# A four-layer decoder: the first projection rotates by a lane shuffle, and the fp4 rounding of all eight weight pieces stands beside it

## What is computed

```python
x = x + _L0_attn_ref(_layernorm(x), Wq, Wk, Wv, Wo)          # 16 heads of 32, 8 key heads
#   q = q * cos + _rotate_half(q) * sin ; k likewise
#   att = 50 * tanh(q k^T / 16 / 50), causal, softmax, times v, times Wo
x = x + _L0_xattn_ref(_layernorm(x), ctx, ctx)
x = x + _L0_ffn_ref(_layernorm(x), up_kernel, up_bias, down_kernel, down_bias)

def quantize_to_mxfp4(w, block_size=32):     # blocks of 32 along K
    amax = max(abs(block)); scales = exp2(floor(log2(max(amax, 1e-30))) - 2)
    idx = digitize(abs(w / scales), [0.25, 0.75, 1.25, 1.75, 2.5, 3.5, 5.0])
    q = sign(w / scales) * [0, .5, 1, 1.5, 2, 3, 4, 6][idx]
    return q, scales                          # the matmul uses q * scales
```

## Time and profile before

| | us |
|---|---|
| median of 3 runs (1390.68 to 1394.52) | 1392.82 |
| the profiled execution | 1394.05 |
| its span | 1392.3 |
| TensorE busy | 1239.9 (89%) |
| VectorE busy | 817.3 (59%) |
| ScalarE busy | 526.3 (38%) |
| GpSimd busy | 329.8 (24%) |
| load of the fp4 kernels, issue to landing (2560 KB) | 16.9 |

### The profile page before, as it was taken

One profiled execution on the slowest core, in us unless ns is written; L12 is line 12 of the kernel. 1 busy time (PEld: TensorE's weight loads), 2 busy tenths in 40 slices (PEclk: granted clock), 3 DMA queues, 4 the chain that ended last, 5 costly groups with the idle time before them and its releaser, 6 DMA issues. The chain is left out here.

```text
span 1392.3 us, 23432 instructions
## 1 busy us (share of the span) xinstructions
PE 1239.9 (89%) x9322; PEld 744.2 (53%) x9334; DVE 817.3 (59%) x2109; ACT 526.3 (38%) x967; POOL 329.8 (24%) x364
## 2 busy tenths in 40 slices
PE   5678779788999899899998998999999999994898
PEld 2246554456854544556664544555555555663455
DVE  2887767757687344768766766343111126777955
ACT  1019335563524433544444545111111114445453
POOL 0225502100003100245542221232222223450200
PEclk9688899998999999999999999999999999996999
DMA  9000000000040030000000000123232210000000
GB/s 384 1 0 3 1 1 2 0 1 1 1 197 2 10 112 1 1 2 3 3 2 1 2 2 1 52 75 95 80 106 80 84 37 1 2 3 0 1 1 31
DMA packets 13340, 48.02 MB, mean 34 GB/s; under 512 B 1688, under 2 KB 4888, under 8 KB 12464
## 3 DMA queue, kind: packets, MB, share of 16 engines
q1 hardware_dynamic: 13232, 46.53, 10.0%
HBM read 45.37 MB, written 1.15 MB: 33 GB/s over the span
## 5 line engine op out<-in xcount | busy, mean ns | idle before, releaser
L821 ACT ACTIVATE PT<-PS 128x384 f32<-128x384 f32 (+1 forms) x320 | 153.2, 531 | 189.3 <-PE PS L631 138.4
L1930 PE MATMUL PS<-HT,WA 128*128 128x512 f32 x448 | 201.5, 593 | 2.4 <-DVE MO L2008 2.0
L2008 DVE TENSOR_TENSOR MO<-PS,AO 128x512 f32<-128x512 f32 x56 | 38.7, 690 | 205.9 <-ACT AO L1998 205.8
L1930 PEld LDWEIGHTS PS<-HT,WA 128*128 128x128 f32 x448 | 84.7, 190 | 87.7 <-issue 82.9
L1998 ACT ACTIVATE AO<-PS 128x512 f32<-128x512 f32 x56 | 33.3, 597 | 247.9 <-PE PS L1930 247.9
L757 DVE CUSTOM_DVE_ANT_0 junk<-PS,TRI 128x128 bf16<-128x128 f32 (+1 forms) x384 | 112.6, 352 | 4.0 <-PE PS L612 0.2
L1938 PE MATMUL PS<-WA,HO 128*128 128x256 f32 x448 | 105.6, 378 | 0.0
L1938 PEld LDWEIGHTS PS<-WA,HO 128*128 128x128 f32 x448 | 84.5, 189 | 34.7 <-issue 24.9
L240 PE MATMUL PS<-identb 128*128 128x512 bf16 x388 | 99.2, 394 | 3.2 <-PEq L584 1.2
L2063 POOL TENSOR_TENSOR HO<-MO,GR 128x512 f32<-128x512 f32 x44 | 57.8, 1314 | 168.7 <-PE PS L1938 168.7
L612 PE MATMUL PS<-KS,QM 32*128 32x128 f32 (+1 forms) x768 | 86.7, 347 | 7.5 <-DVE QM L791 6.6
(11 more groups left out here) (323 smaller groups left out, 2412.8 us busy)
## 6 DMA issues: line engine op xcount, KB each, us to landing
WA<-w2f_in SPq DMA_DIRECT2D x28, 384.0 KB, 4.5
WA<-wl_in SPq DMA_DIRECT2D x1, 5137.0 KB, 16.0
GR<-gate_rows SPq DMA_DIRECT2D x20, 256.0 KB, 3.9
GB<-gate_rows SPq DMA_DIRECT2D x8, 512.0 KB, 7.4
WA<-wa_in SPq DMA_DIRECT2D x2, 1792.0 KB, 12.2
WB<-wb_in SPq DMA_DIRECT2D x1, 3208.0 KB, 18.4
WA<-wa_in SPq DMA_DIRECT2D x1, 2560.0 KB, 16.9
GR<-gate_rows SPq DMA_DIRECT2D x4, 448.0 KB, 4.0
```

The costliest lines, as they stand in the source:

```text
L821: act.activation(PT[:, g % 3, st_slot(k), 0:W], PS[:, st_bank(g, k), 0:W], ACT.Exp, scale=scale).then_inc(S["at_exp"], 1)
L1930: last = pe.matmul(PS[:, 2 * c + half, :], chunk(i, half)[:, k * P:(k + 1) * P], HT[:, k, c * CH:(c + 1) * CH], start=k == 0, stop=k == KD ...
```

## The change

The swapped weights are gone. In `project` TensorE computes each item once; VectorE takes it from PSUM with a shuffle that exchanges the two halves of each 32 lanes into RS, and multiplies it by the cosines into RC; GpSimd multiplies RS by the sines and adds. RC, RS and the PSUM banks of the items have four buffers. The products for V stand between the items from the third on, and GpSimd's wait for `b_in` stands behind its work.

All eight pieces are rounded in `project`. VectorE takes the largest magnitudes behind items 1 to 3 and forms all powers at once in four small instructions; ScalarE writes absolute values into H; with item m + 4 VectorE scales piece m and makes four of the seven comparisons, each into a bf16 tile of its own (0, 0.5, 1 or 2), and GpSimd makes the other three; TensorE sums the seven tiles by products with the identity (two items later); VectorE has put signs and powers together (one item later) and multiplies the sums by them, to bf16. The rounded pieces are turned by 32 bf16 products in the tail of the stage and copied by ScalarE. The attention keeps its own work alone, and the cross-attention has no kernel head, so that it takes the branch with the 24 `warm` matmuls.

The core of the diff:

```diff
@@ project, TensorE @@
-                    for n, (a, ap, _, j, c) in enumerate(work):
+                    for n, (a, _, j, c) in enumerate(work):
                         if n < NCH:
                             norm["columns"](pe, 2 * n + 1)
-                        if n >= 2:
-                            pe.wait_ge(S["rope_sin"], d["rope_sin"] + n - 1)
-                        for half, wt in enumerate((a, ap)):
+                        if n >= 4:
+                            pe.wait_ge(S["rope_pair"], d["rope_pair"] + n - 3)
+                            pe.wait_ge(S["rope_cos"], d["rope_cos"] + n - 3)
+                        for k in range(KD):
+                            last = pe.matmul(PS[:, n % 4, :], a[:, k, j * P:(j + 1) * P],
+                                             HT[:, k, c * CH:(c + 1) * CH], start=k == 0, stop=k == KD - 1)
+                        last.then_inc(S["proj"], 1)
+                        t = n - 2
+                        if 0 <= t < TT:
...
+                        kernels["tensor"](pe, n, NW)
@@ project, VectorE @@
-                        dve.tensor_tensor(tm(RC), ps(0), cos.to_broadcast([P, nchunk, T]), ALU.mult).then_inc(S["rope_cos"], 1)
-                        dve.tensor_tensor(tm(RS), ps(1), sin.to_broadcast([P, nchunk, T]), ALU.mult).then_inc(S["rope_sin"], 1)
+                        if n >= BUF:
+                            dve.wait_ge(S["rope_sum"], d["rope_sum"] + n - BUF + 1)
+                        dve.stream_shuffle(RS[:, n % BUF], ps, PAIR[hd]).then_inc(S["rope_pair"], 1)
+                        dve.tensor_tensor(wide(RC[:, n % BUF]), wide(ps), cos.to_broadcast([P, nchunk, T]),
+                                          ALU.mult).then_inc(S["rope_cos"], 1)
+                        kernels["vector"](dve, n, NW)
@@ project, GpSimd @@
+                        pool.tensor_tensor(wide(RS[:, n % BUF]), wide(RS[:, n % BUF]), sin.to_broadcast([P, nchunk, T]),
+                                           ALU.mult).then_inc(S["rope_sin"], 1)
+                        pool.wait_ge(S["rope_sin"], d["rope_sin"] + n + 1)
+                        pool.wait_ge(S["rope_cos"], d["rope_cos"] + n + 1)
+                        pool.tensor_tensor(dst[:, j, c * CH:(c + 1) * CH], RC[:, n % BUF], RS[:, n % BUF], ALU.add).then_inc(S["rope_sum"], 1)
+                        kernels["beside"](pool, n, NW)
                     pool.wait_ge(S["b_in"], 64)
@@ quantise_fp4 @@
+        STEPS = [(5.0, 2.0), (3.5, 1.0), (2.5, 1.0), (1.75, 0.5), (1.25, 0.5), (0.75, 0.5), (0.25, 0.5)]
+        OWN = 4
+        def largest(dve, m):
+            if m == 0:
+                dve.wait_ge(S["kernels_in"], 16)
+            dve.tensor_reduce(per(0, m), grp(piece(order[m])), AX, ALU.max, apply_absolute_value=True).then_inc(S["q_largest"], 1)
+        def scaled(dve, m):
+            dve.wait_ge(S["q_sizes"], m + 1)
+            v = grp(at["scaled"][:, m % 4])
+            dve.tensor_tensor(v, v, wide(per(2, m)), ALU.mult).then_inc(S["q_scaled"], 1)
+        def sizes(act, m):
+            if m >= 4:
+                act.wait_ge(S["q_steps"], OWN * (m - 3))
+                act.wait_ge(S["q_steps_beside"], (len(STEPS) - OWN) * (m - 3))
+            act.activation(at["scaled"][:, m % 4], piece(order[m]), ACT.Abs).then_inc(S["q_sizes"], 1)
+        def signed(dve, m):
+            dve.scalar_tensor_tensor(u32(grp(at["signed"][:, m % 2])), u32(grp(piece(order[m]))), 0x80000000, u32(wide(per(1, m))), ALU.bitwise_and,
+                                     ALU.bitwise_or).then_inc(S["q_signed"], 1)
+        def steps_of(eng, m, lo, hi, name):
+            eng.wait_ge(S["q_scaled"], m + 1)
+            if m >= 2:
+                eng.wait_ge(S["q_summed"], m - 1)
+            for j in range(lo, hi):
+                eng.tensor_scalar(at["steps"][:, m % 2, j, :], at["scaled"][:, m % 4], STEPS[j][0], STEPS[j][1], ALU.is_ge, ALU.mult).then_inc(S[name], 1)
+        def summed(pe, m):
+            pe.wait_ge(S["q_steps"], OWN * (m + 1))
+            pe.wait_ge(S["q_steps_beside"], (len(STEPS) - OWN) * (m + 1))
+            for j in range(len(STEPS)):
+                last = pe.matmul(PS[:, 6 + m % 2, :], identb[:], at["steps"][:, m % 2, j, :], start=j == 0, stop=j == len(STEPS) - 1)
+            last.then_inc(S["q_summed"], 1)
+        def kept(dve, m):
+            dve.wait_ge(S["q_summed"], m + 1)
+            dve.wait_ge(S["q_signed"], m + 1)
+            dve.tensor_tensor(rounded(m), PS[:, 6 + m % 2, :], at["signed"][:, m % 2], ALU.mult).then_inc(S["q_kept"], 1)
...
+            if n == last - 1:
+                pe.wait_ge(S["ctx_copied"], TT // 2)
+                for g in range(4):
+                    turned_over(pe, g)
+                for m in range(early - 2, early):
+                    summed(pe, m)
+                for g in range(4, 8):
+                    turned_over(pe, g)
@@ capped_attention, VectorE @@
-                        beside(dve, g, NQ)
@@ layers @@
-        cross_attention(32, norm=norm, head=kernels)
+        cross_attention(32, norm=norm)
```

More of the change, by code:

```diff
@@ new lines, in quantise_fp4, with begin @@
+        at = {}
+        rounded = lambda m: piece(order[m]).bitcast(BF16)[:, 0:CH]
+        def begin(tmp):
+            at.update(scaled=H[:].rearrange("p (j t) d -> p j (t d)", j=4), signed=tmp("SP", [P, 2, CH]), steps=tmp("IND", [P, 2, 7, CH], BF16),
+                      small=tmp("SM", [P, 3, early * NG]))
+        STEPS = [(5.0, 2.0), (3.5, 1.0), (2.5, 1.0), (1.75, 0.5), (1.25, 0.5), (0.75, 0.5), (0.25, 0.5)]
+        OWN = 4
+        per = lambda j, m: at["small"][:, j, m * NG:(m + 1) * NG]
@@ L2476, in column_of, with gqa @@
     return v.reshape(-1, P).T
[L2479 to L2487 removed]
+def gqa(wq, wk, wv, wo, hd, group):
     if hd == 32:
```

283 lines of the change are left out of this document (132 added, 151 removed).

## The result

| | before | changed |
|---|---|---|
| median of 20 runs | 1394.96 us | 1390.01 us |
| lowest to highest | 1390.68 to 1400.27 | 1387.14 to 1392.22 |
| span of the profiled run, granted clock | 1392.3 us, 0.953 | 1386.5 us, 0.956 |

The ratio is 0.9963, with a 95% interval of 0.9953 to 0.9972: faster by some 5 us, where 31 us were forecast. The direction came true, the size did not, and the time lies outside the range of 1346 to 1378.

The account below looks back on a forecast made before the run. Three stages in sequence were taken as bounds: VectorE in the projection, ScalarE with late GpSimd in the attention, kernel turning at the cross attention's head. Gains of 20.1 + 7.2 + 3.5 = 30.8 us gave 1362.0, range 1346 to 1378.

Parts of the forecast that it names:

- Up to item 4: Projection's start: item 0 ready at 17.4 us, items 1 to 3, maxima and small steps done on VectorE at 28.97.
- the choice of the cheaper of two rows: Projection: VectorE's comparison from fp32 into bf16 priced at 0.48 us, not 0.74, which would cost 8 us over eight items.
- three comparisons at 0.78: Projection: price in us of each GpSimd comparison, three an item, giving GpSimd about 5.0 us an item.
- rival 4: Projection: GpSimd comparisons cost a multiple; no gain from 2.4 us each, 1406 at 3; chance 0.04 with other slower cases.
- Term A: Projection stage: the next stage starts at 82.3 instead of 102.4 us, a gain of 20.1.
- rival 1: Projection: engines share rather than overlap, 7.6 us an item, gain 10, time 1372; chance 0.17 together with a cold TensorE.
- The 6.4: Projection: us taken per item carrying a piece, between 5.1 (GpSimd decides) and 7.6 (VectorE always meets GpSimd).
- Term B: Capped attention: with VectorE's fp4 work gone, shorter waits and a kept TensorE clock gain 7.2 us, between 2 and 10.
- Should keep its clock: Attention's second block: TensorE, idling about 2 us instead of 4.46, stays at full clock, worth 1.8 us.
- Term C: Cross attention's head: first exponential at 197.95 instead of 201.49, a gain of 3.5 us, from 0 to 5.
- At half clock it would be busy without a pause: Projection: TensorE needs 8.1 us an item at half clock, so constant work would bring its full clock back.
- rival 3: Attention: the stalls are GpSimd's own order and stay, gain 2, time 1368; counted within the 0.54 for 1354 to 1370.

Follow-up runs that it names:

- e2: The changed kernel with GpSimd's three comparisons a piece replaced by multiply-adds (a measurement, no candidate): 1374.26 us.
- e6: e3 with GpSimd's sine product and add cut to 16 columns, ScalarE copying the cosine part instead (a measurement, no candidate): 1363.6 us.
- e3: The changed kernel with all seven comparisons on VectorE, none on GpSimd: 1374.2 us.
- e10: e9 with VectorE's product with the sums, which reads PSUM, moved ahead of scaling and comparisons: 1362.9 us.
- e12: The changed kernel with GpSimd comparing only, the weight of 0.5 moved into the identity through which TensorE sums: 1385.07 us.
- e8: The kernel of before without the fp4 steps beside the capped attention (a measurement, no candidate): 1389.5 us.
- e5: The changed kernel with GpSimd's three comparisons given to ScalarE, four staying on VectorE: 1367.74 us.
- e9: e5 with the context's transposes one item earlier and the first pieces turned ahead of the last three sums: 1363.28 us.
- e1: The kernel of before with ten unused one-operand GpSimd instructions put in while it waits for the last load: 1394.96 us in one run.
- e4: The changed kernel with six comparisons on VectorE and one on GpSimd: 1377.06 us.
- e11: e9 with four comparisons on ScalarE and three on VectorE: 1363.0 us.

## Why the prediction was wrong

**Up to item 4: right.** Item 0 was ready at 16.8 (17.4 forecast), item 4 began at 29.3 (28.97). GpSimd started without its old wait. VectorE's comparison into bf16 is 0.43, so the choice of the cheaper of two rows was right.

**The step that failed** is "three comparisons at 0.78, bounded below by the simple add of L1068 at 1.27 on two operands and by L2425". The row was of the right engine, width and operand count, but of another operation, multiply-and-add. The comparisons measured 1.94 to 2.16 each in the mean of a piece. The sentence on rival 4, "no one-operand GpSimd row of this width exceeds 1.0", was true and worthless: besides L2425 only the causal masks are such rows (0.86 and 0.64 us), and none of them is a comparison with a multiplication. Rival 4's own arithmetic works: 24 comparisons x (2.0 - 0.78) = 29.3, less GpSimd's spare time of 8, is 21.3. Term A came out 24.8 below its forecast (-4.7 instead of +20.1); the rest is that the eight groups of three take 49.9 us instead of 48 (1.9) and the longer tail (1.8). Terms B and C together missed by another 1.6. The mechanism was named and priced, with a chance of 0.04. For an operation without a row, a range from 0.78 to 3 us would have been honest: its middle, 1.9, gives some 1381 by the same sum, and its end the 1406 of rival 4.

**The second failure lies under the first.** With GpSimd as fast as assumed (e2) an item is 7.2 us, not 6.4, and the time 1374. VectorE's nine instructions are 4.45 undisturbed (e6's 5.49 less three comparisons at 0.35); the scaling adds 0.55 and the four comparisons 2.2. That is rival 1, "the engines share rather than overlap", at 7.6 and 1372. The 6.4 was chosen between 5.1 and 7.6 on the thought that GpSimd meets VectorE only part of the time. But the schedule makes them meet: each item GpSimd starts behind the shuffle, and so runs beside the scaling and the comparisons, the two that it stretches. That can be read from the order ahead of any run. What can't be read from it is who waits: in e3, e10 and e12 it was the instruction that began second. e10 shows the reverse order: one instruction moved, and the scaling is undisturbed.

**Term B** was right in the waits and wrong in the clock. The three waits of TensorE shrank by 1.1, 2.6 and 1.1 us, 4.7 in all, where 1.0 + 2.5 + 1.0 = 4.5 were forecast. The clock was to give 1.8 + 0.9 and gave about 0.5: the third block came back to full clock (2.5), the second did not (0.2 of the 1.8), and the first lost it (1.6), with 0.5 lost ahead of it. That the sum of 5.3 (5.6 in e8) lies near 7.2 - 2.7 is in part luck, since no sign of the first block's loss was seen. "Should keep its clock" was no safe step: behind waits of the same 1.9 us some blocks were at full clock and some at half, and in e3 none kept full clock and the attention took 76.1 us. **Term C** came out at 3.8 (3.5 forecast), by the fill and the score as forecast; that the fill could be left out at this place changes 1.1 us.

**TensorE's clock.** "At half clock it would be busy without a pause, which is what has brought the clock back" could not come true, since TensorE waited 32.9 us for GpSimd. (Rows 1 hold one window and show no return of the clock.) In e5 and e9, with items of 5.98, the windows from 40 to 60 have a granted clock of 0.94 and 0.99.

**Slips in the sums.** 2 x 1.27 + 0.08 is 2.62, not 2.65, and rival 3's B of 2 gives 1367, not 1368. Neither changes the forecast.

## What to carry to other kernels

A duration is a price only for the operation that was measured: when a profile has one row for an engine's operation and the change uses another, take the range from a multiple of it, and let that range reach the total, above all where the instruction stands in the chain of every item. Before two engines are made to share work, write down which instructions will run at the same time by the order itself, and take their durations from rows where the two met. And look first for an engine that is idle: the three comparisons on ScalarE instead of GpSimd took 22 us off the change, which is over four times what the change itself had gained.

## What was unexpected about the hardware

- GpSimd, 128x512, one operand, VectorE idle or reading PSUM (e1): multiply-and-add 0.62 us; a single multiplication or comparison 1.50; the three other pairs tried 1.92 or 1.93; compare-and-multiply with its constants per partition 2.08. A single multiplication is 2.4 times as long as a multiplication with an addition.
- VectorE turns fp32 into bf16 by a comparison every 0.35 us when undisturbed (seven in 2.44, e6), every 0.75 beside GpSimd's multiply-and-adds (e2), every 0.5 in the mean beside GpSimd's slow comparisons. It goes both ways: GpSimd's single comparison went from 1.50 to as much as 2.06 (e12).
- An instruction that reads PSUM was stretched in none of the rows read here.
- VectorE's scaling, with two SBUF inputs, and GpSimd's product or add took turns: whichever began first kept its length. The scaling was 1.23 with 0.68 of the product still to run (e3), 1.68 with 1.13 of the add (e12), each time that rest and 0.55. It was 0.67 where it began before the add, and then the add took 1.65 (e10). Beside GpSimd's slow comparisons the scaling did not wait, although they had begun first: 0.68 in the changed kernel.
- Behind a wait of 1.9 us TensorE was at full clock in some blocks of the attention and at half in others, in kernels whose attention is the same code; its length went from 73.5 (e12) to 76.1 us (e3 and e4). A gain of 1 or 2 us in one profile can be that alone.

The best of these kernels, e9 to e11, take 1363 us, a ratio of 0.977 to the kernel of before. Which of the three is fastest can't be told.
